# The decayed state of a gated delta-rule chain made on ScalarE, with ScalarE's other work cut into new pieces

## The reference

```python
q = q / norm(q) / sqrt(DH); k = k / norm(k)
def step(S, inp):                      # S: [b, h, 8, 8] per sequence and head
    k_t, q_t, v_t, beta_t, a_t = inp
    S = S * a_t[..., None, None]
    kv_mem = einsum('bhd,bhde->bhe', k_t, S)
    delta = (v_t - kv_mem) * beta_t
    S = S + k_t[..., :, None] * delta[..., None, :]
    y_t = einsum('bhd,bhde->bhe', q_t, S)
    return S, y_t
ctx = rmsnorm(ys, norm_w) * silu(gate)
x = layernorm(x + ctx @ Wo.T + bo)
```

## Time and profile before

| | us |
|---|---|
| median of 3 runs | 789.41 |
| lowest and highest | 789.19, 790.91 |
| span of the profiled execution (first to last instruction) | 785.4 |
| median less span: what lies around the instructions | 4.0 |
| VectorE busy | 632.3 (81%) |
| GpSimd busy | 601.7 (77%) |
| TensorE matmul busy | 659.5 (84%) |
| ScalarE busy | 415.3 (53%) |

### The profile page before, as it was taken

How to read it: one execution, slowest core, us unless ns; L and a number is a source line. 1 busy time by engine, 2 the same in 40 slices (tenths; PEclk the granted TensorE clock), 3 DMA queues, 4 the chain that set the end, 5 groups by cost and what they waited for, 6 DMA issues and landing times.

```text
span 785.4 us, 13851 instructions
## 1 busy us (share of the span) xinstructions
PE 659.5 (84%) x3513; PEld 502.7 (64%) x3513; DVE 632.3 (81%) x1701; ACT 415.3 (53%) x1313; POOL 601.7 (77%) x758
## 2 busy tenths in 40 slices
PE   8778699898989889999998978576689878999980
PEld 3445374755747556574654746465579778999980
DVE  3899999999999999999999999996953525666430
ACT  6736455656566546655556566233224335666651
POOL 2888797989999999999999999996733354444673
PEclk9879798989999999898999999788759989999996
DMA  6833233351433416333262432217254456677630
GB/s 172 198 95 97 65 101 87 80 151 53 128 102 89 129 54 148 92 100 96 83 155 64 116 91 74 71 37 268 67 176 150 148 179 203 230 239 235 212 116 5
DMA packets 135919, 97.28 MB, mean 124 GB/s; under 512 B 95630, under 2 KB 110225, under 8 KB 135714
## 3 DMA queue, kind: packets, MB, share of 16 engines
q1 hardware_dynamic: 130514, 87.55, 38.7%
q0 software_dynamic: 4320, 8.43, 3.3%
q10 hardware_dynamic: 1008, 0.43, 0.2%
HBM read 39.80 MB, written 31.43 MB: 91 GB/s over the span
## 4 chain that ended last, share of the span: by engine, by line
PE 33%; DVE 32%; POOL 17%; issue 7%; ACT 6%; DMA 1%; another core or an unknown queue 1%; DVEq 0%; ACTq 0%; POOLq 0%
PE banks L434 11%; DVE banks L1903 6%; PE banks L447 5%; DVE banks L1877 5%; DVE upd L1891 5%; POOL q_prod L1308 4%; DVE prod L1861 4%; DVE banks L1887 3%; DVE mix L1881 3%; PE banks L750 3%; POOL u L1308 2%; DVE upd L1872 2%; PE banks L674 2%; POOL solve L1308 2%; POOL x_sorted L346 2%
## 5 line engine op out<-in xcount | busy, mean ns | idle before, releaser
L1308 POOL TENSOR_TENSOR q_prod<-s_keep,q_gam 128x512 f32<-128x512 f32 x128 | 140.7, 1100 | 16.5 <-ACT s_keep L1006 9.0
L1006 ACT ACTIVATE s_keep<-banks 128x128 f32<-128x128 f32 x128 | 50.3, 393 | 170.1 <-DVE upd L1891 164.1
L750 PE MATMUL banks<-q_prod,ident 128*128 128x240 f32 (+1 forms) x496 | 113.7, 384 | 20.8 <-POOL q_prod L1308 20.7
L750 PEld LDWEIGHTS banks<-q_prod,ident 128*128 128x128 f32 x496 | 94.6, 195 | 41.2 <-POOL q_prod L1308 30.3
L434 PE MATMUL banks<-xs_t,w_tile 128*128 128x128 f32 x852 | 111.6, 282 | 8.6 <-issue 5.1
L543 POOL DMA_INDIRECT out<-rows_out,xs x71 | 70.1, 987 | 60.3 <-ACT rows_out L524 51.6
L1903 DVE TENSOR_REDUCE banks<-upd 128x128 f32<-128x640 f32 x128 | 105.7, 826 | 7.4 <-DVE upd L1891 0.5
L434 PEld LDWEIGHTS banks<-xs_t,w_tile 128*128 128x128 f32 x852 | 104.8, 198 | 10.3 <-issue 7.5
L578 DVE TENSOR_TENSOR hid<-banks,silu 128x384 f32<-128x384 f32 x71 | 39.6, 557 | 71.9 <-PE banks L434 39.6
L1877 DVE TENSOR_REDUCE banks<-prod 128x64 f32<-128x576 f32 x128 | 93.7, 732 | 0.0
L1861 DVE TENSOR_TENSOR prod<-banks,k_gam 128x512 f32<-128x512 f32 x128 | 88.3, 690 | 3.4
(11 more groups left out here) (224 smaller groups left out, 1481.1 us busy)
## 6 DMA issues: line engine op xcount, KB each, us to landing
w_tile<-gate_up_we SPq DMA_DIRECT2D x71, 352.0 KB
xs<-x_sorted SPq DMA_DIRECT2D x71, 64.5 KB, 1.9
x_ct<-in_x_ct SPq DMA_DIRECT2D x16, 256.0 KB, 2.9
k_dram<-kq_s SPq DMA_DIRECT2D x16, 256.0 KB, 2.9
q_dram<-kq_s SPq DMA_DIRECT2D x16, 256.0 KB, 3.8
out<-v_s SPq DMA_DIRECT2D x16, 256.0 KB, 2.6
out<-beta SPq DMA_DIRECT2D x16, 256.0 KB, 3.5
k_h<-k_dram SPq DMA_DIRECT2D x16, 256.0 KB, 3.3
```

The lines of the kernel that those rows point to most:

```text
L750: i = mm(out, ident[:, :], q_prod[m][:, d, :, 1 - m:], start=(m == 0 and d == 0), stop=(d == DH - 1), skip_group_check=True)
L1308: b.step(label, win, lambda: tt(out, x, y, op))
```

## The change

1. Step 2 leaves VectorE. ScalarE makes it: `fade` in the new `serve(g)`, two copies of 64 columns with the chunk's decay as the scale of each partition, one for each sequence of the pair.
2. `serve(g)` takes the place of `keep(g)`: it waits for `s_prod` at g + 1 (step 1), then runs `fade` and `s_keep` of chunk g, and then the deltas of chunk g - 1 (`deltas`).
3. Key sums and deltas are written to the other bank. `cand`/`before` and `top`/`place_f` of the routing change banks too.
4. VectorE's key-sum reduce takes the waits that stood at step 2 and two more, for `s_keep` of chunk g - 1 and `d_keep` of chunk g - 2. The state reduce waits for `fade` of its own chunk where it waited for `d_keep` of the last. `s_upd` now counts one for each chunk.
5. ScalarE's blocks are cut otherwise between the eight calls, `decay_of` goes ahead of the gates, and `y_square` goes behind the fourth call.
6. Routing steps 3, 4, 8 and 9 move by one place in VectorE's chunks.

```diff
-            def keep(g):
+            def deltas(g):
+                win, c = g // NCH, g % NCH
+                to = d_keep[win % 2][:, :, 0:C - 1, c] if win < NW - 1 else d_last[:, :, 0:C - 1, c]
+                from_d = chain_ps[(g + 1) % 2][:, P:P + 64].rearrange("p (n j) -> p n j", j=C)[:, :, 0:C - 1]
+                b.wait(pool, "y_prod2", win - 2)
+                b.step(f"d_keep{c}", win, lambda: A(to, from_d, ACT.Copy))
+
+            def serve(g):
...
-                b.wait_chunks(s_upd, 2 * g + 2)
+                b.wait_chunks(s_prod, g + 1)
+                if c == 0:
+                    b.wait(pool, "gam3", win)
+
+                def fade():
+                    for i in range(2):
+                        last = A(upd[:, :, C].rearrange("p (e b d) -> p e b d", e=DH, b=2)[:, :, i, :],
+                                 bank[:, 0:P].rearrange("p (e b d) -> p e b d", e=DH, b=2)[:, :, i, :],
+                                 ACT.Copy, scale=decays[win % 2][:, i, 3, c:c + 1])
+                    return last
+                b.step(f"fade{c}", win, fade)
                 b.wait(pool, f"q_prod{(g - 4) % NCH}", (g - 4) // NCH)
                 b.step(f"s_keep{c}", win, ...)
-                b.step(f"d_keep{c}", win, ...)
+                if g:
+                    deltas(g - 1)
...
             if b.last:
-                keep(NCH * w - 1)
+                serve(NCH * w)
                 variance(o)
                 log_root(o)
                 x1(o)
-                keep(NCH * w)
+                serve(NCH * w + 1)
                 fill(4 * w + 1)
-                keep(NCH * w + 1)
+                serve(NCH * w + 2)
                 y_square()
                 x1_turned(o)
...
-                keep(NCH * w + 5)
+                serve(NCH * w + 6)
+                serve(NCH * w + 7)
                 variance(p)
                 log_root(p)
                 x1(p)
-                keep(NCH * w + 6)
+                b.wait(dve, "y_ends", w)
+                deltas(NCH * w + 7)
                 x1_turned(p)
-                keep(NCH * w + 7)
                 router_logits(p)
...
-                if b.route and c == 6 and k == 4:
-                    route_part(r, 8)
-                if b.route and c == 7 and k == 0:
-                    route_part(r, 9)
+                if b.route and c == 7 and k < 2:
+                    route_part(r, 8 + k)
...
-                bank, after = chain_ps[g % 2], chain_ps[(g + 1) % 2]
+                bank, other = chain_ps[g % 2], chain_ps[(g + 1) % 2]
-                delta = bank[:, P:P + 64].rearrange("p (n j) -> p n j", j=C)
-                k_s = bank[:, P + 64:P + 128]
+                delta = other[:, P:P + 64].rearrange("p (n j) -> p n j", j=C)
+                k_s = other[:, P + 64:P + 128]
...
-                    v.tensor_tensor(upd[:, :, C].rearrange("p (e b d) -> p e b d", e=DH, b=2), s_in,
-                                    decays[par][:, :, 3, c].unsqueeze(1).unsqueeze(3).to_broadcast([P, DH, 2, DH]),
-                                    ALU.mult).then_inc(s_upd, 1)
-                if live:
+                    if g:
+                        b.wait(act, f"s_keep{(g - 1) % NCH}", (g - 1) // NCH)
+                        b.wait(act, f"d_keep{(g - 2) % NCH}", (g - 2) // NCH)
                     e.wait_ge(s_prod, g + 1)
                     v.tensor_reduce(k_s, pr, AX, ALU.add).then_inc(s_read, 1)
...
-                    if g:
-                        b.wait(act, f"d_keep{(g - 1) % NCH}", (g - 1) // NCH)
-                    e.wait_ge(s_upd, 2 * g + 2)
-                    v.tensor_reduce(after[:, 0:P], upd[:, :, :], AX, ALU.add).then_inc(s_state, 1)
+                    b.wait(act, f"fade{c}", w)
+                    e.wait_ge(s_upd, g + 1)
+                    v.tensor_reduce(other[:, 0:P], upd[:, :, :], AX, ALU.add).then_inc(s_state, 1)
```

More of the change, by code:

```diff
@@ L203, in block_kernel @@
         down_mean = side[:, 3 * P + 2 * TW:3 * P + 2 * TW + IC * E]
-        cand, before = (chain_ps[n][:, 2 * P:2 * P + TW * E].rearrange("p (t e) -> p t e", e=E) for n in range(2))
-        top, place_f = (chain_ps[n][:, 3 * P:3 * P + TW] for n in range(2))
+        cand, before = (chain_ps[n][:, 2 * P:2 * P + TW * E].rearrange("p (t e) -> p t e", e=E) for n in (1, 0))
+        top, place_f = (chain_ps[n][:, 3 * P:3 * P + TW] for n in (1, 0))
         s_iota, s_wexp = sem("s_iota"), sem("s_wexp")
@@ L1007, in keep @@
                                                     bank[:, 0:P].rearrange("p (n d) -> p n d", d=DH), ACT.Copy))
-                to = d_keep[win % 2][:, :, 0:C - 1, c] if win < NW - 1 else d_last[:, :, 0:C - 1, c]
-                b.wait(pool, "y_prod2", win - 2)
-                b.step(f"d_keep{c}", win, lambda: A(to, bank[:, P:P + 64].rearrange("p (n j) -> p n j", j=C)[:, :, 0:C - 1], ACT.Copy))
+                if g:
+                    deltas(g - 1)
             def fill(pair):
@@ L1201, in act_body @@
                 y_root()
-                keep(NCH * w + 3)
-                keep(NCH * w + 4)
+                serve(NCH * w + 4)
+                serve(NCH * w + 5)
                 fill(4 * w + 3)
-                keep(NCH * w + 5)
+                serve(NCH * w + 6)
+                serve(NCH * w + 7)
                 variance(p)
@@ L1233, in act_body @@
                 return
-            keep(NCH * w - 1)
+            if b.chain:
+                serve(NCH * w)
+            if b.pre:
+                decay_of(n)
             if b.load:
@@ L1243, in act_body @@
                 b.step("tanh", a, lambda: A(beta[:, :], pre_ps[:, 0, :], ACT.Tanh, scale=0.5))
+            if b.chain:
+                serve(NCH * w + 1)
+                fill(4 * w + 1)
+            if b.load:
                 b.wait(pe, "z", a)
@@ L1251, in act_body @@
             if b.pre:
-                decay_of(n)
                 q_squares(n)
-            keep(NCH * w)
             if b.chain:
-                fill(4 * w + 1)
+                serve(NCH * w + 2)
             if b.load:
@@ L1279, in act_body @@
                 b.step("k_r", a, lambda: A(k_sq[:, :], k_sq[:, :], ACT.Exp, scale=-0.5))
+            if b.chain:
+                serve(NCH * w + 4)
             if b.post:
                 y_root()
-            keep(NCH * w + 4)
-            if b.chain:
-                fill(4 * w + 3)
             if b.pre:
@@ L1287, in act_body @@
                 solve_ends(n)
+            if b.chain:
+                serve(NCH * w + 5)
+                fill(4 * w + 3)
             if b.out:
@@ L1318, in q_times_s @@
                     b.wait(act, "q_next", win - 1)
+                    b.wait(pool, "q_gam", win)
                 if c == 1:
@@ L1468, in pool_body @@
                 b.wait(act, "alpha", n)
-                b.wait_chunks(s_upd, 2 * NCH * w)
+                b.wait(act, f"fade{NCH - 1}", w - 1)
                 decay_powers(n)
```

35 lines of the change are left out of this document (13 added, 22 removed).

## The result

The changed kernel is **slower**, by 0.8%: 796.24 us (median of 5 runs, 795.92 to 798.57) against 789.41 (5 runs, 785.28 to 790.91) on the same chip. The ratio is 1.0084, with a 95% interval of 1.0052 to 1.0115. The prediction said 785.7 and gave 0.18 to slower.

What follows compares the result with a forecast made beforehand. VectorE's chain was taken as the bound, GpSimd close behind. Gains of 0.84 (windows 0 to 2), 1.92 (3 to 14) and 0.96 (last) make 3.7: span 785.4 to 781.7, plus 4.0 gives 785.7 us; range 780.5 to 790.5.

Steps and rivals of the forecast that it cites:

- at 0.79 after `prod`'s start: VectorE's key-sum reduce, each chunk: would start there, with the state reduce's gap of 0.10; gain taken as 0.035 a chunk.
- the case of more among the bounds: VectorE's key-sum reduce: three semaphores instead of two could cost more than 0.10 and leave no gain.
- the wait costs what the multiply cost: Rival at the key-sum reduce: three semaphores put it at 0.82 again, no gain a chunk, 790.1; chance 0.14.
- Moved routing steps "nothing": VectorE's chunks: routing steps 3, 4 and 8 land in places empty or holding one, and cost nothing.
- The third rival: TensorE's loop becomes the bound at VectorE's first `y_n`, chunk 4, windows 3 to 14: slower than before; chance 0.16.
- my lateness of 0.97: ScalarE's LayerNorm block: `x1_turned` behind chunk 6's call is 0.97 late, with `router` behind it; hidden, 0.46 left.
- 0.12 was foreseen: VectorE, chunk 7, windows 3 to 14: a second small operation between `mix` and its reduce adds about 0.12.
- some 2 us late: Last window: `y_square`, behind chunk 2's call, is late, bringing `y_root` about to `y_n`; 0.15 of waiting counted.
- `turn` should be 0.9 sooner: End of the last window: `turn` starts at 569.8 instead of 570.67, about 0.9, which the tail passes on.
- predicted 0.38 and 0.67: ScalarE: a pair of `fade` takes 0.38 us, a whole `serve` with `s_keep` and `d_keep` 0.67.
- The free wait: Rival: key-sum reduce at 0.72, gaining 0.105 a chunk, capped by spares of 0.43 (GpSimd) and 0.46; 778.4; chance 0.08.

Runs made afterwards that it cites:

- e10: The changed kernel with only the order of waits changed: VectorE's own wait named first at both reduces; ratio 0.9892.
- e15: The kernel of e14 with the multiply of state and decay back on VectorE, behind the big product; ratio 0.9852.
- e14: The kernel of e12 with two instead of three of GpSimd's indirect DMAs a window, the rest issued behind the last `ctx`; ratio 0.9754.
- e5: The changed kernel with four added TensorE matmuls of 512 columns ahead of `count`, whose results nobody reads; ratio 1.0200.
- e2: The changed kernel with routing steps 3 and 4 both behind the key-sum reduce of chunk 2, so `one_hot` comes sooner; ratio 1.0082.
- e4: The changed kernel with `y_square` ahead of the work for chunk 2 in the last window; ratio 1.0008.
- e7: The kernel before with, in its last window, ScalarE's `keep` of chunk 6 ahead of the last `variance` and of chunk 7 ahead of `x1_turned`; ratio 1.0001.
- e12: The changed kernel with key-sum reduce's ScalarE waits moved to the state reduce, e4's edit, old routing places, and VectorE's own waits named first; ratio 0.9825.
- e9: The kernel of e12 with the multiply of state and decay back on VectorE; ratio 0.9883.
- e6: The changed kernel with the multiply back on VectorE; `serve` waits for it, and the state reduce no longer waits for `fade`; ratio 0.9969.

## Why the prediction was wrong

- **The failing step** is the key-sum reduce "at 0.79 after `prod`'s start". It took the state reduce's gap of 0.10 as the price of a second semaphore and put the case of more among the bounds. The reduce had three semaphores or more, and 0.824 came. What the step had wrong is where the price lies: not in a second semaphore as such, but in VectorE's own wait, named last and so met in a separate instruction (e10: 0.725 with all of them). Of the rivals the second, "the wait costs what the multiply cost", named the 0.82, by the number of semaphores, and so the size but not its reason.
- **A term was missing**: the reduce's length. Right behind the multiply it lasts 0.73, without it 0.76 (e15 against e14). This 0.03 turned no gain a chunk into a loss of 0.02. With the step above it makes 120 x (0.035 + 0.024) = 7.1 of the 12.7 us by which the span missed the predicted 781.7. The rest: 4.8 for the stalls of chunk 4, 3.3 in the last window, 0.3 of hiccups, less 0.6 in chunk 7 and 2.1 at the end, which both came better than predicted.
- **Moved routing steps "nothing"**: wrong for step 4. `one_hot` a little later cost VectorE nothing, but TensorE's `count` waited for it (13.9 us over twelve windows; before, 2.6 over six), and behind that idle time the granted clock stood at 0.5 for a part of `kkqk` (mean 0.68). e5 shows the link (no idle time, no slow `kkqk`) and e2 agrees (0.2 to 1.0 us in eleven windows and 1.45 in window 14, one slow of twelve); idle time alone doesn't settle it, as window 6 of the changed kernel and window 14 of e2 show. The third rival had the right loop and victim, priced at 0.16, but what came late was `count`, behind `one_hot`: my lateness of 0.97 for `x1_turned` and `router` never bound. For chunk 7, 0.12 was foreseen (0.60 from `mix` to its reduce) and 0.07 came (0.54).
- **The last window**: `y_square` "some 2 us late" was right (2.2 came), but 0.15 for it was wrong; I followed it to `y_root` alone, not to TensorE, where `count` stands behind the mean square. It cost 4.0; e4 took all of it back.
- **The end**: `turn` should be 0.9 sooner against chunk 7's `prod`, and is 0.8 (581.87 - 577.39 = 4.48, against 570.67 - 565.43 = 5.24). (The prediction's own terms add up to 569.7, not 569.8.) The whole end was 3.0 shorter, 2.1 more than predicted. In the kernel before, e7's move made the profiled end 2.3 shorter, which the time didn't confirm; where the 2.1 came from stays open.
- **ScalarE** was priced right. From its start to the next instruction's a pair of `fade` took 0.41 and a `serve` 0.68 (predicted 0.38 and 0.67; to their own ends 0.58 and 0.89), and ScalarE's busy time grew by 50 us, 0.39 a chunk. No VectorE instruction waited for one in the changed kernel, as predicted.
- **The free wait** (rival one: the key-sum reduce at 0.72, chance 0.08) is what e10 reached: 0.725. The runs show it where VectorE's own wait stands on the instruction itself (0.725 with one semaphore or seven), and not where it stands on the one ahead (0.79 to 0.82). The cap that this rival put on the gain, GpSimd's spare, was real as well: e10, e12 and e9 ran into it.

## What to carry to other kernels

Name the wait that is met last, on a chained engine its own, first, so that it sits on the instruction, and let the waits that are long met sit ahead of it (here both reduces then started at 0.725, where the other order gave 0.79 to 0.82); then count what a wait costs from a gap in the trace with the same order, not the same number. An instruction that hides a wait is worth keeping until the wait is gone: moving it away alone gained nothing here (0.828 before, 0.824 after, and a reduce 0.03 longer). When the chain gets faster, read the next engine's stream per window (here GpSimd's, busy for 32.1 of 33.5 us) and the idle times of TensorE that a moved producer opens.

## What was not expected of the hardware

A reduce of 576 elements a partition takes 0.73 us right behind a short independent multiply, 0.755 with a semaphore instruction between (e6), and 0.76 without the multiply (e14); which bank it writes makes no difference (e15 and the kernel before both 0.73). Why, no run shows. Sixteen matmuls of 256 columns took 3.7 or 5.4 us in the same place of different windows, mostly 5.4 where TensorE had been idle for 1.1 us or more shortly before, mostly 3.7 where for 0.9 or less. Of the windows in between, and of those with the same 1.2 us, some were slow and some not: e4 has three windows of 3.7 behind 1.2.
